# AdaLN block with retention attention: the modulation weights are loaded as f32 by ScalarE's queue in 24 slices instead of by GpSimd's casting queue in 12

## What is computed

```
mod = silu(c) @ wmod                      # wmod is 1024 x 6144, f32
sa, ca, ga, sb, cb, gb = mod in 6 rows of 1024 ; ga, gb get a floor of 0.25 on their size
h = layernorm(x) * (1 + ca) + sa
x = x + ga * retention(h)                 # q, k, v = h @ W.T ; decayed q k^T v ; norm over (d, t) ; @ W_o.T
h = layernorm(x) * (1 + cb) + sb
x = x + gb * ffn(h)                       # 64 small channels of width 16
```

## Time and profile before

| | us |
|---|---|
| median of 2 runs | 1033.98 (1032.57 to 1035.4) |
| the profiled execution | 1044.03 |
| its span on the slowest core (core 2) | 1042.5 |
| spans of the other cores | 1021.0 to 1038.2 |
| start to the transpose kT(1) | 269.5 |
| kT(1) to kT(7), six chunks | 191.0 |
| from kT(7) to the end | 582.0 |

### The profile page before, as it was taken

The page is one execution under the profiler, slowest core; times in us unless marked ns, Lnnn a source line. Parts: engine busy times, 40 slices in busy tenths (PEclk is TensorE's granted clock), DMA queues, the critical chain, the costliest instruction groups (busy, mean ns, idle before and its releaser), DMA issues.

```text
span 1042.5 us, 8306 instructions; the slowest of 8 cores (1021.0 to 1042.5 us)
## 1 busy us (share of the span) xinstructions
PE 483.8 (46%) x2518; PEld 210.3 (20%) x2518; DVE 394.1 (38%) x677; ACT 216.6 (21%) x339; POOL 47.7 (5%) x86
## 2 busy tenths in 40 slices
PE   0302013044276655767777676544444455344441
PEld 0000001011132222324333343111111111111110
DVE  0100401032365656547567565343222333322331
ACT  1000201021113133133434411011121121122121
POOL 5010010100000000000000000000000000000000
PEclk9755557566588787788888877666656656666655
DMA  7667698595644312222232321011211121211121
GB/s 108 114 107 101 94 148 121 101 147 95 105 88 91 71 41 34 48 51 51 51 77 64 64 52 21 0 50 52 60 51 51 64 67 61 60 51 51 53 69 30
DMA packets 124827, 73.35 MB, mean 70 GB/s; under 512 B 105470, under 2 KB 117808, under 8 KB 124272
## 3 DMA queue, kind: packets, MB, share of 16 engines
q1 hardware_dynamic: 103680, 33.57, 16.9%
q0 software_dynamic: 18800, 30.87, 16.3%
q10 hardware_dynamic: 2304, 8.39, 2.6%
HBM read 60.62 MB, written 16.78 MB: 74 GB/s over the span
## 4 chain that ended last, share of the span: by engine, by line
DMA 32%; DVE 30%; PE 16%; issue 10%; ACT 8%; POOL 2%; DVEq 1%; SPq 1%; ACTq 0%; POOLq 0%
DVE sqs L193 7%; PE ps L533 6%; DVE h L193 6%; DMA kfm<-ktm 5%; DMA hT<-h 5%; ACT qtm L768 4%; DMA wsc<-wk 4%; DMA wsc<-wo 4%; DMA wsc<-wv 4%; DVE st L193 4%; DMA wsc<-wq 4%; DMA wmsl<-wmod 3%; DMA ybf<-wmod 2%; DVE x L193 2%; DVE xa L193 2%
## 5 line engine op out<-in xcount | busy, mean ns | idle before, releaser
L639 PE MATMUL ps<-wt_o,ybf 128*128 128x512 bf16 x256 | 89.2, 511 | 49.0 <-DVE x L193 42.2
L193 DVE SCALAR_TENSOR_TENSOR xa<-psY,x 128x1024 f32<-128x1024 f32 x16 | 19.6, 1225 | 189.4 <-PE psY L671 189.4
L193 DVE TENSOR_TENSOR st<-psS,mask_sb 128x512 bf16<-128x512 f32 x64 | 44.3, 692 | 117.9 <-PE psS L557 112.2
L533 PE MATMUL ps<-wt_v,hT 128*128 128x512 bf16 x256 | 61.1, 387 | 49.5 <-DMA wt_v<-wsc 49.5
L533 PE MATMUL ps<-wt_q,hT 128*128 128x512 bf16 x256 | 82.2, 492 | 0.0
L768 ACT ACTIVATE qtm<-psS,b1pp_sb,wp_sb 128x128 bf16<-128x128 f32 x128 | 46.3, 467 | 119.7 <-PE psS L653 119.7
L490 PE MATMUL ps<-ybf,silb_sb 128*1 128x512 bf16 x64 | 24.7, 555 | 94.8 <-DMA ybf<-wmod 94.8
L710 ACT ACT_TABLE_LOAD x16 | 20.5, 1283 | 227.2 <-DVE var L193 227.2
L533 PE MATMUL ps<-wt_k,hT 128*128 128x512 bf16 x256 | 59.5, 387 | 9.5 <-DVE qtm L193 9.5
L653 PE MATMUL psS<-hT,windup 128*128 128x128 bf16 x128 | 16.1, 305 | 90.2 <-DMA hT<-h 90.2
L557 PE MATMUL psS<-qfm,kfm 64*128 64x128 bf16 x256 | 23.0, 232 | 73.8 <-DMA kfm<-ktm 53.8
(11 more groups left out here) (128 smaller groups left out, 638.3 us busy)
## 6 DMA issues: line engine op xcount, KB each, us to landing
xa<-x ACTq DMA_DIRECT2D x16, 512.0 KB, 3.5
ybf<-wmod POOLq DMA_DIRECT2D x8, 1024.0 KB, 11.5
xa<-x POOLq DMA_DIRECT2D x16, 512.0 KB, 3.6
out<-xa SPq DMA_DIRECT2D x16, 512.0 KB, 2.6
wmsl<-wmod POOLq DMA_DIRECT2D x4, 1024.0 KB, 11.9
wsc<-wq POOLq DMA_DIRECT2D x8, 256.0 KB, 4.5
wsc<-wk POOLq DMA_DIRECT2D x8, 256.0 KB, 5.5
wsc<-wv POOLq DMA_DIRECT2D x8, 256.0 KB, 4.6
```

What stands on the lines that cost most here:

```text
L193: ins = getattr(v, name)(*a, **kw)
L533: mm = t.matmul(ps01[:, 512 * hf:512 * (hf + 1)], hT[p][:, 128 * dc:128 * (dc + 1)], wt[nm][:, 1024 * dc + 512 * hf:1024 * dc + 512 * (hf ...
L639: t.matmul(ps01[:, 512 * hf:512 * (hf + 1)], ybf[:, 1024 * tau + 128 * dj:1024 * tau + 128 * (dj + 1)], wt["o"][:, 1024 * dj + 512 * hf:10 ...
```

## The change

- `wmod` goes in 24 slices of 256 columns. `SLICE_ORDER` lists them so that the columns come in the same order as before.
- A slice is loaded uncast, as f32, by two plain transfers of 512 KB from ScalarE's queue: rows 0 to 511 of `wmod` into `x2_0`, rows 512 to 1023 into `x2_1`. Before each, ScalarE waits for the landing of the last slice and for its gemv (`t_gemv`): there is one pair of buffers.
- The gemv has 8 matmuls on 256 columns with both operands f32 (`silf_sb` instead of `silb_sb`); the two copies and the spreading matmul are on 256 columns.
- Steps 0 to 7 stand ahead of the first `v_pre`, and steps 2c + 8 and 2c + 9 at the head of chunk c, c = 0 to 7.
- GpSimd's queue has no `wmod` transfers: the 32 casts stand one behind another. `wmsl` is gone and `ybf` is free of slices.
- On ScalarE the square root of chunk 0 moves behind the square of chunk 1, the x load of chunk c + 3 behind the copies of v of chunk c, and the two waits for `t_gemv` at chunks 8 and 12 go.

```
-    def wmv(s): ...                                   # three buffers, s % 3
-                vop("tensor_copy", mrow_sb[0:1, :], ps4[0:1, :], mark=("mrow", s))
+                vop("tensor_copy", mrow_sb[0:1, 0:256], ps4[0:1, 0:256], mark=("mrow", s))
-            for s_i in range(4):
+            for s_i in range(8):
                 mod_step_v(s_i)
...
-                    mod_step_t(c + 4)
+                    mod_step_t(2 * c + 8)
+                    mod_step_t(2 * c + 9)
...
-                    mm2 = t.matmul(ps4[0:1, :], silb_sb[:, dc:dc + 1],
-                                   wten[:, wbase + 512 * dc:wbase + 512 * (dc + 1)],
+                    mov = x2[0] if dc < 4 else x2[1]
+                    mm2 = t.matmul(ps4[0:1, 0:256], silf_sb[:, dc:dc + 1],
+                                   mov[:, 256 * (dc % 4):256 * (dc % 4 + 1)],
...
+            def wm_load(s):
+                j = SLICE_ORDER[s]
+                if s >= 1:
+                    sc.wait_ge(S["s_wm0"], 16 * s)
+                    sc.wait_ge(S["t_gemv"], s)
+                wsrc = wmod_d[:, :].rearrange("(c p) o -> p c o", c=NDC)
+                sc.dma_start(x2[0][:].rearrange("p (c o) -> p c o", c=4),
+                             wsrc[:, 0:4, 256 * j:256 * (j + 1)]).then_inc(S["s_wm0"], 16)
+                if s >= 1:
+                    sc.wait_ge(S["s_wm1"], 16 * s)
+                sc.dma_start(x2[1][:].rearrange("p (c o) -> p c o", c=4),
+                             wsrc[:, 4:8, 256 * j:256 * (j + 1)]).then_inc(S["s_wm1"], 16)
...
-            sc_rho(0)
+            for s_i in range(8):
+                wm_load(s_i)
             sc_tab(1)
             sc_sq(1)
+            sc_rho(0)
             sc_rho(1)
             x_load(2)
+            wm_load(8)
+            wm_load(9)
+            wm_load(10)
             for c in range(KB_NCH):
                 p = c % 2
-                if c + 3 < KB_NCH:
-                    x_load(c + 3)
...
+                if c + 3 < KB_NCH:
+                    x_load(c + 3)
+                if 11 <= 2 * c + 11 <= 23:
+                    wm_load(2 * c + 11)
                 if c + 2 < KB_NCH:
                     sc_rho(c + 2)
-                if c == 8:
-                    sc.wait_ge(S["t_gemv"], 11)
-                if c == 12:
-                    sc.wait_ge(S["t_gemv"], 12)
+                if 11 <= 2 * c + 12 <= 23:
+                    wm_load(2 * c + 12)
```

More of the change, by code:

```diff
@@ L23 @@
 KB_ST7 = 3
-SLICE_ORDER = [0, 1, 2, 3, 4, 5, 10, 11, 6, 7, 8, 9]
+SLICE_ORDER = [0, 1, 2, 3, 4, 5, 6, 7, 8, 9, 10, 11,
+               20, 21, 22, 23, 12, 13, 14, 15, 16, 17, 18, 19]
 def _consts():
@@ L116, in build_nc @@
     wt = {n: A(f"wt_{n}", [128, NDC * D], BF16) for n in ("q", "k", "v", "o")}
-    wmsl = A("wmsl", [128, NDC * 512], BF16)
     modt = A("modt", [128, 6 * D], BF16)
@@ L162, in build_nc @@
     ps7 = nc.alloc_psum_tensor("ps7", [128, 512], F32)
[L164 to L168, removed]
     sem_names = [
@@ L172, in build_nc @@
         "s_wtq", "s_wtk", "s_wtv", "s_wto",
-        "s_xa0", "s_xa1", "s_wm0",
+        "s_xa0", "s_xa1", "s_wm0", "s_wm1",
         "s_hT0", "s_hT1", "s_qT0", "s_qT1", "s_kT0", "s_kT1",
@@ L210, in mod_step_v @@
                     v.wait_ge(S["t_mod"], s)
-                vop("tensor_copy", mrow_sb[0:1, :], ps4[0:1, :], mark=("mrow", s))
+                vop("tensor_copy", mrow_sb[0:1, 0:256], ps4[0:1, 0:256], mark=("mrow", s))
                 v.wait_ge(S["t_mod"], s + 1)
-                vop("tensor_copy", modt[:, 512 * j:512 * (j + 1)], ps4[:, 0:512],
+                vop("tensor_copy", modt[:, 256 * j:256 * (j + 1)], ps4[:, 0:256],
                     mark=("modp", s))
@@ L255, in _ @@
                 if 0 <= c <= 7:
-                    mod_step_v(c + 4)
+                    mod_step_v(2 * c + 8)
+                    mod_step_v(2 * c + 9)
                 v.wait_ge(S["sc_tab"], c + 1)
@@ L483, in mod_step_t @@
                 t.wait_ge(S["s_wm0"], 16 * (s + 1))
+                t.wait_ge(S["s_wm1"], 16 * (s + 1))
                 if s >= 1:
                     t.wait_ge(S["vp"], vpos[("modp", s - 1)])
-                if s == 11:
+                if s == 22:
                     t.wait_ge(S["vp"], vpos["bfh0"])
-                wten, wbase = wmv(s)
                 for dc in range(NDC):
-                    mm2 = t.matmul(ps4[0:1, :], silb_sb[:, dc:dc + 1],
-                                   wten[:, wbase + 512 * dc:wbase + 512 * (dc + 1)],
+                    mov = x2[0] if dc < 4 else x2[1]
+                    mm2 = t.matmul(ps4[0:1, 0:256], silf_sb[:, dc:dc + 1],
+                                   mov[:, 256 * (dc % 4):256 * (dc % 4 + 1)],
                                    start=(dc == 0), stop=(dc == NDC - 1))
@@ L494, in mod_step_t @@
                 t.wait_ge(S["vp"], vpos[("mrow", s)])
-                t.matmul(ps4[:, 0:512], ones_sb[0:1, :], mrow_sb[0:1, :],
+                t.matmul(ps4[:, 0:256], ones_sb[0:1, :], mrow_sb[0:1, 0:256],
                          start=True, stop=True).then_inc(S["t_mod"], 1)
-            for s_i in range(4):
+            for s_i in range(8):
                 mod_step_t(s_i)
@@ L503, in _ @@
                 if 0 <= c <= 7:
-                    mod_step_t(c + 4)
+                    mod_step_t(2 * c + 8)
+                    mod_step_t(2 * c + 9)
                 if c == 6:
                     t.wait_ge(S["vp"], vpos["ffn1"])
-                    t.wait_ge(S["vp"], vpos[("modp", 10)])
+                    t.wait_ge(S["vp"], vpos[("modp", 21)])
                     t.matmul(ps4[0:1, 0:512], b2b_sb[:, 0:1],
@@ L512, in _ @@
                     t.wait_ge(S["vp"], vpos["bfh0"])
-                    t.wait_ge(S["vp"], vpos[("modp", 11)])
+                    t.wait_ge(S["vp"], vpos[("modp", 23)])
                     t.matmul(ps4[0:1, 0:512], b2b_sb[:, 0:1],
@@ L806, in _ @@
             ).then_inc(S["s_cst"], 16)
[L808 to L818, removed]
             def wcast(i, wd):
@@ L825, in wcast @@
                                 wd[128 * oc:128 * (oc + 1), :]).then_inc(S[f"s_wc{i}"], 16)
-            wm_load(0); wm_load(1)
             wcast(0, wq_d)
-            wm_load(2); wm_load(3)
             wcast(1, wk_d)
-            wm_load(4); wm_load(5)
             wcast(2, wv_d)
-            wm_load(6); wm_load(7)
             wcast(3, wo_d)
-            for s_i in range(8, 12):
-                wm_load(s_i)
             if KB_PH3:
```

## The result

The changed kernel takes 1070.26 us in the median of 11 runs (1065.89 to 1074.33), the kernel before 1036.37 in 10 runs beside it. The ratio is 1.0314, with a 95% interval of 1.028 to 1.0347: slower by 3.1%. I had forecast 1049, called that inside 2%, "near the edge", and given "same" 0.44 and "slower" 0.42. The time lies inside my range of 1010 to 1095, the call was wrong.

What follows compares the result with a forecast made beforehand. It took chains of waits as the bound: GpSimd's transfers up to 264 us, then engine-to-engine waits in the loop. -13.7 us ahead of kT(1) and +28.5 in six chunks gave +14.8, 1048.8 on the median; range 1010 to 1095.

Steps and rivals of the forecast that it cites:

- The two sums and their places: Time until k's transpose kT(1) is issued, forecast -13.7 us; six chunks from there to kT(7), +28.5; nothing after.
- The turn of the prologue: Prologue: slice landing 9.3, f32 gemv 5.2, semaphores and issue 0.3, so 14.8 us a turn, eight turns ending at 143.9.
- Two more turns, 188.3: Prologue: chunk 0 needs steps 8 and 9 before its q matmuls, two turns to 188.3, q(0) at 189.3.
- The v weights "8 x 2.64": Prologue: transposes that need not wait for pieces take 2.64 us each, the eight for v 21.1 us, v(0) at 220.
- One chunk of the loop, 36.1 us: Chunk loop, from one k transpose to the next: q starts at +27.3 instead of +19.8, and kT follows 8.8 later.
- The second slice lands at 14.25 + 6.9 = +21.2, and this is what ends last: Chunk loop: the second slice's load, not `modt` (written at +20.7), releases the chunk's second gemv.
- the sum of 219.5: Chunk loop: six chunks at 216.6 us plus extras for `wt_o` and ffn, 219.5 against 191.0, a loss of 28.5.
- the serial turn is longer: Rival, prologue and loop: one buffer pair makes longer landing and gemv add up, 1082 to 1122 us; chance 0.28.
- Shared casts: Rival, prologue: casts and slices share the DMA engines, kT(1) comes where it was, 1062.5 us; chance 0.10.
- The short turn: Rival, prologue and loop: landing 6.5 and gemv 3.6 make a turn of 10.4, 999 us; chance 0.17.

Runs made afterwards that it cites:

- k_first: Changed kernel with the transposes of the k weights ahead of hT(0) on SyncE's queue; 1075.54 us, ratio 1.035 to the kernel before.
- root_first: Changed kernel with ScalarE's square root ahead of the first load of a chunk in the loop; 1066.33 us, ratio 1.0282 to the kernel before.
- two_steps: Kernel before, bf16, loads and buffers untouched, each step computed as two halves of 256 columns one behind the other; 1057.48 us, ratio 1.0203.
- half_gemv: Changed kernel with 4 of the 8 f32 matmuls of each gemv, half of the product left out; 1044.56 us, ratio 1.0056 to the kernel before.
- two_pairs: Changed kernel with a second pair of f32 buffers, a load waiting for the gemv before the last; 1040.01 us, ratio 1.0024 to the kernel before.
- f32_wide: Like the changed kernel, but 12 f32 slices of 512 columns, four buffers, one step per chunk, load behind the square of psY; 1004.07 us, ratio 0.9659.

## Why the prediction was right and wrong

**The two sums and their places**: right. All of the difference lies ahead of kT(1) and between kT(1) and kT(7); the rest moved by 1.2 us.

**The turn of the prologue** (14.8 us; eight turns to 143.9; load 8 at 158.7): right, 143.8 and 158.67 on core 7. That it fits to 0.1 us is luck: single landings scatter, and on the mean of the cores hT(0) moved by 36.4 us where the sum has 38.8. The f32 gemv, forecast as 5.2 from the weight loads of rows 6 and the clock of rows 7, took 4.9 to 6.4 in those eight turns; the landing of the first slice was 10.2 and the others on the chain 7.0 to 11.3, where I took 9.3.

**"Two more turns, 188.3"**: failed, by 10 us on core 7: q(0) at 199.4. On the mean of the cores q(0) moved from 153.7 to 190.8, 37.1 us where I had 31.1. I had counted the k transposes as ready before q(0), which they are, but not that they go out at the moment at which slice 8 is issued. k_first shows that this traffic cost as much where that run put it. **The v weights "8 x 2.64"** was wrong the other way: the 2.64 came from a stretch with casts beside them; behind the last cast a transpose takes 11.03 / 8 = 1.4 us. The two nearly cancel: kT(1) gained 10.1 instead of 13.7.

**One chunk of the loop, 36.1 us**: measured 37.6 for the one shown, 38.6 on the mean of all. The step that failed is "The second slice lands at 14.25 + 6.9 = +21.2, and this is what ends last". What ends last is the square root, held back by its queue position, and VectorE behind it: `modt` is ready at +22.1, in the chunk shown, and releases the second gemv in 48 of 48 cases; the load is next in line, as root_first shows. The steps that I had written down for that chain were the right ones, and their terms were too small, in order: the first gemv 4.8 us instead of 3.95, the two issues and their hand-over 1.1 instead of 0.7, which brings the root to +16.0 instead of +14.9; then the second gemv 5.54 instead of 5.2, its hand-over to q 1.1 instead of 0.9. q starts at +28.9 instead of +27.3, and the chunk is 1.5 us longer than forecast. Six times that is 9 of the 12 us that the sum of 219.5 lacked against 231.5. The other 3 lie in the chunks from kT(4) on (38.5, 39.5 and 38.5 us, where the first two took 37.6 and 37.7). On core 7 the two gemvs at kT(4) take 5.14 and 5.78 us, and at kT(5) two things hold q that I had not counted there: VectorE's work on the ffn weights, which brings the root to +16.6, and an ffn matmul that waits for `modt` and sets q back by 1.1. So the term that was mis-sized is the serial pair of steps in the loop, forecast to cost 28.5 us and measured at 41.9.

The 9.1 us by which q starts later in the chunk shown are told by the runs as follows: two_steps gives 3.3 for a second step as such (1.87 of gemv and its copies); the f32 gemv behind `v_pre` is longer by 5.54 - 1.87 = 3.7; the root starts 2.1 later. 3.3 + 3.7 + 2.1 = 9.1. Less 2.3 for q at the full clock it is 6.8, and that chunk lost 6.9. The first of the three is measured by a run of its own. The other two are read off the trace; half_gemv and root_first bear them out in direction only (2.6 and at most 0.7 us a chunk), since another wait takes over when one is shortened. That six times 6.8 is 41 and the loop lost 41.9 is partly luck, as the chunks lost between 5.0 and 8.3.

The 36.1 was worked out from a chunk with a gate adjustment on VectorE and taken for all six. It did no harm, as the first gemv and not VectorE sets the root in most of them.

**The rivals**: "the serial turn is longer" is what came, in the loop rather than in the prologue. I had written that 0.4 us more in a turn decides, and gave that 0.28; with a sum of two opposite terms so near the edge, that rival and the call "same" were not separable from these rows. "Shared casts" did not come in the changed kernel (the last cast is issued at 198) and did in two_pairs. The short turn did not come.

**What stays open**: the scatter of the landings between cores (slice 8 needed, by core, 10 to 19 us from its issue to the gemv), and how the 21 us that the loop lost beyond two_steps divide between the f32 length, the queue position and the one pair of buffers: no run combines root_first and two_pairs, and none has two bf16 steps with the loads on ScalarE's queue.

## What to carry to other kernels

Count what lies behind the last wait, not how much work there is: a second small step behind a busy engine costs its whole length and every hand-over (3.4 us a chunk in two_steps), while a gemv of 8.0 us, in one piece beside that engine, cost nothing. When a load is put on a compute engine's queue with a wait on another engine, whatever stands behind it in the queue inherits the wait; and where two such waits are near each other, removing one shows the next. More buffers help where the DMA engines have room: at a share of 0.96 the prefetched slices took from the casts most of what they gained; of 38 us at hT(0) 14 were left at kT(1).

## What the runs showed of the hardware that I had not expected

An f32 matmul with one output row leaves two records, and in the changed kernel 16 such records of 256 columns take 4.9 to 6.6 us behind an idle stretch and 4.0 to 5.5 (median 4.7) right behind other matmuls. On 512 columns, in f32_wide, 8 records at a granted clock of 1.00 (2.4 GHz) take 3.60 us, 0.45 each, twice what a bf16 matmul of 512 columns takes there (3.63 for 16): four times per instruction.

On core 7 of the changed kernel a DMA transpose of 128 x 1024 bf16 goes out every 1.4 us (11.03 / 8) behind the last cast and every 3.5 us (27.74 / 8) beside a slice and casts. The second half of a 1 MB slice landed in 5.2 us in the median of all slices, and in 16.8 beside those eight transposes.
